# Last layer, order of TensorE's work: the value products of the preceding group stand between a group's two pairs of turned scores, and the tile products at the group's end

## The reference, cut to what matters

```python
xn = _layernorm(x)
x = x + _L3_attn_ref(xn, ...) + _L3_ffn_ref(xn, ...)

# _L3_attn_ref: 16 heads of 8 columns
qkv = (x @ W_qkv + b_qkv).reshape(b, s, h, 3 * hd)
logits = jnp.einsum('bshd,bkhd->bhsk', q, k) / np.sqrt(hd)
logits = jnp.where(k_pos > q_pos, -jnp.inf, logits)      # causal
out = jnp.einsum('bhsk,bkhd->bshd', softmax(logits), v).reshape(b, s, d)
return out @ W_out + b_out

# _L3_ffn_ref: 8 experts, each token uses its best 2
cw = (one_hot(top_k_idx, E) * top_k_probs[..., None]).sum(axis=1)
for e in range(E):
    h = new_gelu(x_flat @ w1[e].T + b1[e])               # 128 -> 512
    output = output + cw[:, e:e + 1] * (h @ w2[e].T + b2[e])
```

## Time and profile before

| | |
|---|---|
| median of 3 runs | 2458.77 us |
| lowest and highest run | 2456.61 and 2468.96 us |
| span of the profiled execution | 2438.6 us |
| PE busy | 1961.1 us (80%) |
| DVE busy | 1854.7 us (76%) |
| ACT busy | 1448.4 us (59%) |
| POOL busy | 1318.1 us (54%) |

### The profile page before, as it was taken

How to read it: one execution, slowest core, us unless ns; L and a number is a source line. 1 busy time by engine, 2 the same in 40 slices (tenths; PEclk the granted TensorE clock), 3 DMA queues, 4 the chain that set the end, 5 groups by cost and what they waited for, 6 DMA issues and landing times. The chain is left out here.

```text
span 2438.6 us, 32864 instructions
## 1 busy us (share of the span) xinstructions
PE 1961.1 (80%) x10212; PEld 1020.8 (42%) x10212; DVE 1854.7 (76%) x2464; ACT 1448.4 (59%) x2630; POOL 1318.1 (54%) x962
## 2 busy tenths in 40 slices
PE   6797797979797977879857999656688889898876
PEld 5233343433343333335625777532244544454322
DVE  6499999999999999878787888757465555645752
ACT  2676777767777775563546666312566566655655
POOL 5599999989898989322324554327411111111653
PEclk9898999989898988989888999855899998999978
DMA  2354444545444545300200000022222322322211
GB/s 72 99 160 138 155 144 146 150 154 164 140 142 146 157 140 158 123 27 1 85 0 1 0 0 0 5 76 83 82 75 83 108 77 66 92 68 76 57 44 30
DMA packets 150288, 214.84 MB, mean 88 GB/s; under 512 B 30970, under 2 KB 62612, under 8 KB 149524
## 3 DMA queue, kind: packets, MB, share of 16 engines
q1 hardware_dynamic: 146052, 204.72, 27.8%
q0 software_dynamic: 4096, 8.40, 1.3%
HBM read 193.91 MB, written 23.86 MB: 89 GB/s over the span
## 5 line engine op out<-in xcount | busy, mean ns | idle before, releaser
L717 PE MATMUL ps<-m_hC,ident 128*128 128x512 f32 x1024 | 518.0, 651 | 127.7 <-DVE m_hC L1005 127.7
L914 POOL TENSOR_TENSOR m_dBx<-m_du,m_rowB 128x1024 f32<-128x1024 f32 x256 | 604.0, 2391 | 5.9 <-DMA m_rowB<-bc_rows 5.6
L2909 DVE TENSOR_REDUCE a_mx<-ps 128x2 f32<-128x1024 f32 (+2 forms) x320 | 351.6, 1117 | 183.6 <-PE ps L2571 142.5
L2770 ACT ACTIVATE a_pT<-ps 128x512 f32<-128x512 f32 (+2 forms) x640 | 319.8, 553 | 287.2 <-PE ps L2593 279.5
L840 ACT ACTIVATE ps<-m_delta,m_A 128x512 f32<-128x512 f32 x512 | 339.7, 685 | 119.5 <-DVE m_h L996 118.6
L717 PEld LDWEIGHTS ps<-m_hC,ident 128*128 128x128 f32 x1024 | 207.1, 209 | 423.9 <-issue 237.3
L3056 POOL TENSOR_SCALAR_AFFINE_SELECT a_pT<-a_pT 128x512 f32<-128x512 f32 x128 | 81.5, 636 | 472.0 <-ACT a_pT L2770 471.5
L996 DVE TENSOR_TENSOR_SCAN m_h<-ps,m_carry,m_dBx 128x512 f32<-128x512 f32 x256 | 311.2, 1265 | 9.0 <-ACT ps L840 9.0
L996 DVE TENSOR_TENSOR_SCAN m_h<-ps,m_dBx 128x512 f32<-128x512 f32 x256 | 295.9, 1206 | 18.8 <-ACT ps L840 18.2
L924 POOL TENSOR_TENSOR m_hC<-m_h,m_rowC 128x1024 f32<-128x1024 f32 x80 | 194.6, 2433 | 70.4 <-DVE m_h L996 70.0
L1005 DVE TENSOR_TENSOR m_hC<-m_h,ps 128x1024 f32<-128x1024 f32 x176 | 214.9, 1221 | 21.2 <-ACT ps L850 7.2
(11 more groups left out here) (404 smaller groups left out, 3568.8 us busy)
## 6 DMA issues: line engine op xcount, KB each, us to landing
m_rowB<-bc_rows SPq DMA_DIRECT2D x256, 256.0 KB, 4.4
m_rowC<-bc_rows SPq DMA_DIRECT2D x256, 256.0 KB, 4.0
a_w<-in_L3f_w1T SPq DMA_DIRECT2D x39, 256.0 KB, 2.7
a_w<-in_L3f_w2T SPq DMA_DIRECT2D x39, 256.0 KB, 3.4
qk_parts<-a_part SPq DMA_DIRECT2D x24, 256.0 KB
expert_rows<-in_zero_rows SPq DMA_DIRECT2D x39, 128.0 KB, 2.6
a_xs<-expert_rows SPq DMA_DIRECT2D x39, 128.0 KB, 2.3
expert_out<-a_y SPq DMA_DIRECT2D x39, 128.0 KB, 3.3
```

The source lines that it names most:

```text
L717: mm = pe.matmul(ps[:, bankY + c, :], k.ident[:], hC[:, n % NBUF, c, :], start=False, stop=n % NS == NS - 1)
L914: pool.tensor_tensor(dBx[:, n % NBUF], du[:, i % 2, :, chunk(i, x)], rowB[:, n % 4, :].unsqueeze(1).to_broadcast([P, HALF, CH]), ALU.mult) ...
L2770: act.activation(dst, src, ACT.Exp).then_inc(t_read, 1)
L2909: dve.tensor_reduce(mx[:, c % 2, :, es[0]:es[0] + len(es), t, x // CH], src, AX_X, ALU.max)\
```

## The change

In each group of each slot TensorE now issues: first turned pair, first front unit, `sums` of the group before (at group 0 the last group of the combination before), second turned pair, `turn_rows`, second front unit, projections, `down`, burst. No instruction is added or removed. `ring_tables` numbers `DOWN` after the group's front units and projections, and DVE copies the tile's result (`down_done`) there too. The order on ACT, POOL and SP is the same.

```diff
@@ ring_tables
             for j, kt in enumerate(tiles_of(s)):
                 if g == j:
                     add(s_at, ("XT", kt))
-                if g == BURST:
-                    for x in range(2):
-                        add(t_at, ("UP", kt, x))
-                if g == 7 + j:
-                    add(s_at, ("DOWN", kt))
             for i in units[1:]:
                 add(s_at, ("S", s, i))
...
             for bb, part in projected(s, g):
                 project(bb, part)
+            for j, kt in enumerate(tiles_of(s)):
+                if g == 7 + j:
+                    add(s_at, ("DOWN", kt))
+            if g == BURST:
+                for kt in tiles_of(s):
+                    for x in range(2):
+                        add(t_at, ("UP", kt, x))
@@ TensorE
                         for i in units[:1]:
                             score(f, i)
+                        if back and g > 0:
+                            sums(b, g - 1)
+                        if g == 0 and 0 <= b - 1:
+                            sums(b - 1, GROUPS - 1)
+                        if back and len(TU[g]) > 2:
+                            scoreT(b, g, 2)
                         for j, kt in enumerate(tiles_of(s)):
                             if g == j:
                                 turn_rows(kt)
-                            if g == 7 + j:
-                                down(kt)
-                        if back and len(TU[g]) > 2:
-                            scoreT(b, g, 2)
                         for i in units[1:]:
                             score(f, i)
...
                         for x, part in projected(s, g):
                             project(x, part)
-                        if back and g > 0:
-                            sums(b, g - 1)
-                        if g == 0 and 0 <= b - 1:
-                            sums(b - 1, GROUPS - 1)
+                        for j, kt in enumerate(tiles_of(s)):
+                            if g == 7 + j:
+                                down(kt)
@@ VectorE
-                            if g == 7 + j:
-                                down_done(kt)
                         for i in units[1:]:
                             largest(first, i)
...
+                        for j, kt in enumerate(tiles_of(s)):
+                            if g == 7 + j:
+                                down_done(kt)
```

## The result

The changed kernel takes 2444.77 us (median of 7 runs, 2440.04 to 2450.26), the kernel before on the same chip 2461.20 us (7 runs, 2453.46 to 2473.14). The ratio is 0.9939, 95% interval 0.9921 to 0.9957: 15 us less by the ratio, where 4.5 were forecast. That is within the range given.

The account below looks back on a forecast made before the run. TensorE bounds the tile slots, three engines share slots without tiles, and latencies bound the tail. From a median of 2458.8 us, -1.5 for waits (-12.4 + 3.2 + 7.5 + 0.2) and -3 for the clock give about 2455 us, range 2439 to 2473.

Parts of the forecast that it names:

- The wait behind the burst: Tile slots, groups 5 and 6: value products fill part of TensorE's 1.99 us wait, so group 6 begins 0.7 us earlier.
- Tile slots at full clock: Eight tile slots gain 1.3 us each, slots 6 and 10 gain 1.0 each: 12.4 us gained.
- the small waits of groups 4 and 6: Tile slots: a 0.26 us wait of group 6 and a like one of group 4 go, about 0.6 us gained.
- The clock in the tile slots: Seven clock falls near the burst cost 15 us; more than half may stay up: 8 us gained.
- clock kept: Rival: clock stays up after all or nearly all bursts, nothing falls elsewhere; -16.5 us, 2442 us; chance 0.27.
- The tail: Slots 16 and 17: longer groups and triangle waits cost 3.8 us a slot, 7.5 us lost (bounds 2 and 12).
- the 5 for two more falls of the clock: Plain slots and tail: longer waits there, priced at two more clock falls, 5 us lost.
- starved chain: Rival: second pair behind waiting products costs ACT time in slots without `down`, clock falls in 13 to 17; +18 us; chance 0.15.
- groups 5 to 8 in the tail: Slots 16 and 17: each of four groups takes 2.63 us instead of 2.37, +0.25 us each.
- Slots 13 and 15: Groups on the diagonal without cover wait for the triangle: 1.6 us lost each, 3.2 us in all (bounds 0 and 8).
- Slot 2: POOL's scatters hold up group 8's triangle, which comes 1.1 us later with the change: 1.2 us lost.
- 12.4 + 1.0 + 8 = 21.4 us: Slots 3 to 12: 12.4 from waits, 1.0 from slot 3's wait for a tile's weights, 8 from the clock.

Follow-up runs that it names:

- the fill: Order of before, but TensorE does group 5's first front unit four times instead of once in slots 3 to 12; ratio to before 0.9962.
- the complement: New order in slots 1, 2 and 13 to 18 alone, slots 3 to 12 as in the kernel before; ratio to before 1.0035.
- second occasion: Session on another chip: the fill, group 5 alone, and 3 to 12 with 5 to 8 of 16 and 17 or of 13 to 15; before's median 2438.3 us.
- first profile of before: Profiled execution of the unedited kernel before, span 2438.6 us; a second profile of it has span 2453.4 us.
- first occasion: Session on one chip: second profile of before, new order in 3 to 12 (also with `down` ahead of the second front unit) and outside; before's median 2457.7 us.
- third occasion: Session on another chip with the remaining kernels, no profile of before; before's median 2460.0 us.
- the candidate: New order in slots 3 to 12 in all groups, from slot 13 on only in groups 5 to 8, old order in slot 2; ratio to before 0.9876.

## Why the prediction was right, and where it was off

**The wait behind the burst** was foreseen step by step: 1.0 left ahead of the second pair (1.01), 0.45 ahead of the next first pair (0.47).

**Tile slots at full clock.** Predicted 1.3 us a slot, measured 0.9 (46.0 to 45.1). The step behind the burst gave the 0.7 foreseen: from group 5's first pair to group 6's it takes 3.80 us (1970.13 to 1973.93) where it took 4.48. The 0.6 that the small waits of groups 4 and 6 were to bring is 0.2. Slots 6 and 10 were predicted at 1.0, measured some 1.9: the order of before at a clock of 1.00 takes 54.3 to 54.4 there (the fill, and slot 6 of the complement), the change 52.4 and 52.5. Sum 8 x 0.9 + 2 x 1.9 = 11.0 against 12.4, if slots 3, 5 and 9, of which no profile has both orders at full clock, gain as much as the others. That `down` would bring nothing and lose nothing holds: 4.16 us a group in either order.

**The clock in the tile slots was mis-sized.** I had 15 us to gain and took 8. The five profiles with the new order in all of slots 3 to 12 take 488.0 to 491.8 us there, the five with the old order 509.0 to 516.2; the means are 23 apart, and the runs of the kernel with only these slots changed say 24 to 26. Less the 11 of the waits, about 12 are clock (an estimate from these rows). The falls behind the burst went from seven to three or four. In the change's profile they are in slots 3, 5 and 9, and that of slot 5 is as deep as before (0.94). Slots 6 and 10, which I had left out, are at 1.00 in four of the five new profiles and at 0.91 to 0.97 in nine of ten places in the old ones. The rival "clock kept" was the nearer one: it gave 16.5 us, and 15 were measured, though not for its reason alone, since it had nothing fall elsewhere, and the tail did.

**The tail.** Predicted 7.5 us lost in slots 16 and 17 by waits, and a share of the 5 for two more falls of the clock. The profiles have 94.8 and 95.8 us with all of the new order in the change and in its complement, 88.8 alone, against 79.6 to 79.9 in seven of eight with the old order; the two kernels that change only the tail lost 15 and 13 us. The mechanism is the one named, the second pair queued behind products that wait for the triangle. Group 9 of slot 16 in the changed kernel (gather, triangle, products, second pair, exponentials):

```profile
2376.80 0.95 POOL L3065 DMA_INDIRECT l_xn<-expert_out,l_slot  x1 [0.30 <-issue]
2377.76 0.64 POOL L3060 TENSOR_SCALAR_AFFINE_SELECT a_pT<-a_pT 128x512 f32<-128x512 f32 x1
2378.46 1.64 PE L2613 MATMUL ps<-a_pT,l_v 128*9 128x512 f32 x8 [1.92 <-POOL a_pT L3060]
...
2380.03 0.50 PE L2595 MATMUL ps<-a_q,a_k 51*128 51x384 bf16 x2
2380.57 0.87 ACT L2773 ACTIVATE a_pT<-ps 128x384 f32<-128x384 f32 x2 [3.12 <-PE ps L2595]
```

and the same triangle's gather and products before, with the exponentials of the next pair:

```profile
2387.48 0.95 POOL L3061 DMA_INDIRECT l_xn<-expert_out,l_slot  x1 [0.30 <-issue]
...
2389.14 1.05 PE L2611 MATMUL ps<-a_pT,l_v 128*9 128x512 f32 x8 [1.68 <-POOL a_pT L3056]
...
2390.54 1.09 ACT L2770 ACTIVATE a_pT<-ps 128x512 f32<-128x512 f32 x2 [2.18 <-PE ps L2593]
```

The gather stood ahead of the triangle already, and TensorE waited 1.68 for the triangle; now it waits 1.92. What is new is that ACT's next work is queued behind: it waits 3.12 instead of 2.18, and from group 9's first pair to group 10's it takes 4.91 us (2376.20 to 2381.11) instead of 3.91 (2386.21 to 2390.12), within the 0.9 to 1.3 foreseen. The clock falls here too: the products take 1.64 and the pair 0.50. Slot 17, from its first pair to its last value products:

```profile
2393.24 0.39 PE L2593 MATMUL ps<-a_q,a_k 51*128 51x512 bf16 x2
...
2422.31 0.41 PE L2611 MATMUL ps<-a_pT,l_v 128*9 128x128 f32 x8 [0.36 <-POOL a_pT L3056]
```

```profile
2384.93 0.60 PE L2595 MATMUL ps<-a_q,a_k 51*128 51x512 bf16 x2
...
2417.66 0.61 PE L2613 MATMUL ps<-a_pT,l_v 128*9 128x128 f32 x8 [0.27 <-POOL a_pT L3060]
```

That is 29.1 us before and 32.7 after, 3.7 more where 3.8 were predicted. Slot 16 takes 5.9 more (2359.16 to 2393.24, 2344.97 to 2384.93). The last 5.7 of the 15 lie behind the last products, where no instruction moved. Most of it is clock: the 48 matmuls that end the kernel run at 0.85 before and at 0.50 after.

```profile
2424.90:2436.00 11.10, 9.66 (x48) 6.87 (x48) 3.85 (x6) 0.00 (x0) 0.00 (x0) 0.85 0.09 26
```

```profile
2420.90:2436.20 15.30, 15.22 (x48) 10.66 (x48) 3.25 (x6) 0.00 (x0) 0.00 (x0) 0.50 0.06 19
```

They take 4.2 us more. So the waits of the tail were priced about right and its clock too low; how much of the loss inside slots 16 and 17 is wait and how much clock is not separated. The mechanism of the rival "starved chain" is real, in two of its five slots.

At full clock the price of groups 5 to 8 in the tail was also too high: a group takes 2.54 us now (2408.46 to 2411.00) against 2.37, +0.17 instead of +0.25, and the kernel that has only these shows no loss.

**Slots 13 and 15** were to lose 1.6 each. Slot 13 at full clock went from 28.2 to 31.7, but 28.2 is what the old order takes at full clock on the second occasion, twice, and the first profile of before looks like one of that chip. On the first occasion, at the same clock of 0.90, it takes 33.7 and 33.1 us in the old order and 34.0 in the new one. Slots 13 to 15 together vary from 99.7 to 115.7 us over the profiles for one and the same order; the change's 107.6 and its complement's 111.5 lie within that. A loss there is not shown.

**Slot 2** was to lose 1.2. With the new order it takes 51.5 and 52.4 us, with the old one on the first and third occasion 49.7 to 50.5, though the candidate, with the old order, drew 51.6.

Put together by the runs, which hold more executions than the profiles: slots 3 to 12 were forecast at 12.4 + 1.0 + 8 = 21.4 us gained, and 24 to 26 were measured. All the rest was forecast at 3.2 + 7.5 + 1.2 + 5 = 16.9 lost, and 9 to 12 were measured (4 to 14 by the interval). Both halves missed in the same direction, the second by more, which makes 15 of the 4.5. The mechanisms were right; the sizes that missed are the clock, too small in the tile slots, and the losses outside them, too large in total although the tail alone was if anything worse than its price. The measured time lies in the range, but 10 us from the forecast: that is the range's width and no credit to the sum.

## What to carry to other kernels

Move work that is ready into the place where the bound engine waits, and not work that itself waits for a third engine: in front of a step that feeds the other engine, such a wait starves both. The same edit can be right in one stage and wrong in another, so give it a condition by stage. Where the clock falls in short waits, a wait filled is worth more than its length; and before explaining a small difference by profiles, take several profiles of the kernel before, with the time of each, on the chip on which the other kernel ran.

## What I had not expected of the hardware

Repeating finished work in a wait of 2 us made the kernel faster by 0.38% (0.20 to 0.56), and the granted clock is higher with it: 1.00 in five of eight tile slots instead of one, 0.903 instead of 0.897 over the runs. The value products behind the wait take 1.04 us (2.4 GHz) where they took 1.90 (1.2 GHz). More than this one wait bears on the clock: with it left whole and eleven other groups moved, slots 7, 8, 11 and 12 are at 0.96 to 1.00, where the old order has 0.87 to 0.96 in nineteen places of twenty. And one execution of the old order's tail drew 90.2 us at a clock of 0.66, where nine others have 78.6 to 79.9, seven with the old order and two with groups 5 to 8 in the new one: the tail's clock can fall in either order.
